# A fused attention and expert kernel on one core: in the second attention, the first output tile is issued ahead of two projections, the TensorE program is written without a loop, weights are split one step sooner, and VectorE rotates the first four parts by itself

## The reference

```python
q = jnp.einsum('bim,mhd->bhid', x, wq)      # 16 heads of 128, M = 256
k = jnp.einsum('bim,mhd->bhid', x, wk)
v = jnp.einsum('bim,mhd->bhid', x, wv)
q = rope(q)                                  # halves swapped, times sin, added to x times cos
k = rope(k)
s = jnp.einsum('bhid,bhjd->bhij', q * mult, k * mult)
s = s - INFTY_APPROX * mask                  # causal
p = jax.nn.softmax(s, axis=-1)
o = jnp.einsum('bhij,bhjd->bhid', p, v)
r = jnp.einsum('bhid,hdm->bim', o, wo)
```

## Time and profile before

| what | value |
|---|---|
| time, median of 3 runs | 1659.39 us (1657.05 to 1661.87) |
| the profiled execution, its own time | 1657.26 us |
| its span, first to last instruction | 1655.4 us |
| mean granted TensorE clock | 0.977 |
| attention B, first to last instruction of its own | about 745 to 1356 us of the span |
| busy over the span | PE 93%, PEld 80%, DVE 67%, ACT 49%, POOL 39% |

### The profile page before, as it was taken

One profiled execution on the slowest core, in us unless ns is written; L12 is line 12 of the kernel. 1 busy time (PEld: TensorE's weight loads), 2 busy tenths in 40 slices (PEclk: granted clock), 3 DMA queues, 4 the chain that ended last, 5 costly groups with the idle time before them and its releaser, 6 DMA issues. The chain is left out here.

```text
span 1655.4 us, 28360 instructions
## 1 busy us (share of the span) xinstructions
PE 1532.2 (93%) x9400; PEld 1322.7 (80%) x9400; DVE 1102.1 (67%) x2592; ACT 813.9 (49%) x2012; POOL 637.6 (39%) x550
## 2 busy tenths in 40 slices
PE   6699999999799999997999998998999978999998
PEld 4588888888678888876788887887888867888887
DVE  6577777777775555566667776766767787555554
ACT  3366666666542333325656655565666623333332
POOL 2676777776400000006555665565656600000000
PEclk9799999999999999998999999999999999999999
DMA  2100000000010000001443333333342321000001
GB/s 94 54 16 16 17 16 15 16 0 1 1 65 20 20 20 19 0 1 58 121 129 89 103 99 103 103 93 97 103 121 77 94 60 39 20 20 20 19 1 51
DMA packets 33727, 83.18 MB, mean 50 GB/s; under 512 B 3649, under 2 KB 24129, under 8 KB 33601
## 3 DMA queue, kind: packets, MB, share of 16 engines
q1 hardware_dynamic: 33600, 81.62, 16.0%
HBM read 54.34 MB, written 27.26 MB: 49 GB/s over the span
## 5 line engine op out<-in xcount | busy, mean ns | idle before, releaser
L378 POOL TENSOR_TENSOR ab_swapped<-ab_swapped,const 128x512 f32<-128x512 f32 x128 | 164.4, 1285 | 223.6 <-ACT ab_swapped L373 223.6
L1620 DVE TENSOR_TENSOR f_hidden<-ps,f_silu 128x512 f32<-128x512 f32 x128 | 87.7, 689 | 202.0 <-PE ps L116 202.0
L1510 ACT ACTIVATE f_silu<-ps 128x512 f32<-128x512 f32 x128 | 76.3, 598 | 283.0 <-PE ps L116 283.0
L114 PE MATMUL ps<-xh,f_wl 128*128 128x512 f32 x512 | 203.2, 397 | 1.5 <-DVE f_hidden L1620 1.5
L115 PE MATMUL ps<-xl,f_wh 128*128 128x512 f32 x512 | 202.8, 396 | 0.0
L116 PE MATMUL ps<-xh,f_wh 128*128 128x512 f32 x512 | 202.6, 396 | 0.0
L1339 POOL TENSOR_TENSOR ab_qk<-ab_qk,ab_swapped 128x512 f32<-128x512 f32 x128 | 175.2, 1369 | 10.0
L1229 DVE SCALAR_TENSOR_TENSOR x<-ps,ab_inv,x 128x256 f32<-128x256 f32 x256 | 120.0, 470 | 79.7 <-PE ps L116 74.9
L73 POOL TENSOR_TENSOR rstd<-shifted,minus_half 128x4 f32<-128x4 f32 x16 | 17.1, 1066 | 355.8 <-DVE shifted L67 355.7
L1107 ACT ACTIVATE ab_probs<-ab_probs,ab_negmax 128x128 f32<-128x128 f32 (+1 forms) x256 | 114.6, 448 | 76.7 <-DVE ab_negmax L1205 71.9
L626 ACT ACTIVATE aa_probs<-ps,aa_negmax 128x256 f32<-128x256 f32 x256 | 119.4, 473 | 60.4 <-DVE aa_negmax L709 52.8
(11 more groups left out here) (187 smaller groups left out, 4497.7 us busy)
## 6 DMA issues: line engine op xcount, KB each, us to landing
ab_scratch<-ab_squares SPq DMA_DIRECT2D x32, 768.0 KB, 3.3
ab_probsT<-ab_scratch SPq DMA_DIRECT2D x128, 192.0 KB, 3.8
f_stage<-wf_in SPq DMA_DIRECT2D x16, 768.0 KB, 4.2
b_stage<-wb_qkv_in SPq DMA_DIRECT2D x8, 768.0 KB, 5.8
a_stage<-wa_in SPq DMA_DIRECT2D x8, 608.0 KB, 3.7
x<-x_in SPq DMA_DIRECT2D x4, 512.0 KB, 6.9
bo_stage<-wb_out_in SPq DMA_DIRECT2D x8, 256.0 KB, 4.5
out<-x SPq DMA_DIRECT2D x4, 512.0 KB, 2.9
```

The costliest lines, as they stand in the source:

```text
L114: nc.tensor.matmul(out, ll, rh, start=start, stop=False)
L378: return engine.tensor_tensor(by_batch(out), by_batch(src), table(c, rows, col), ALU.mult)
L1620: nc.vector.tensor_tensor(hidden[:, m, :], UP(m), silu[:, m, :], ALU.mult).then_inc(hid_done, 1)
```

## The change

Five edits, all in `attention_b`:

1. In TensorE's `step`, output tile j - 2 is issued ahead of the two projections at j = 2 (at j = 3 nothing moves).
2. TensorE's eight pairs are written out in Python instead of the hardware loop. GpSimd's loop over the pairs is written out too. ScalarE keeps its loop.
3. Weight splits move: ScalarE's three from j = 3 to j = 2 of the same slot, VectorE's from j = 1 of the slots 1, 2 and 3 to j = 3 of the slots 0, 1 and 2.
4. The first four parts (slot 0) go to four PSUM banks of their own (3, 4, 5 and 2) and TensorE does not wait between them. VectorE rotates them without ScalarE: one product with cosines and two crosswise products with sines on 64 rows (`first_rope`). GpSimd subtracts. The waits `rope_read` and `swap_done` on TensorE begin with the fifth part, and the first projection of values waits for `swap_done` 4, since it writes bank 2.
5. In the start-up VectorE splits the first weights ahead of the layer norm's statistics, and the four `first_rope` stand between the pieces of the norm.

```diff
+        FIRST = [c.ps[:, bank, :] for bank in (3, 4, 5, 2)]
...
-                after(pe, rope_read, 4 * n + i - 1)
-                after(pe, swap_done, 4 * n + i - 1)
+                if n > 0:
+                    pe.wait_ge(rope_read, 4 * n + i - 1)
+                    pe.wait_ge(swap_done, 4 * n + i - 1)
...
+                if j >= 2 and not (first and s == 0):
+                    output(*later(it, half, s, -1), j - 2)
                 if j == 2 and not (last and s >= 1):
                     for i in (0, 1):
                         project(*later(it, half, s, 3), i)
-                if j >= 2 and not (first and s == 0):
-                    output(*later(it, half, s, -1), j - 2)
...
+            pe.wait_ge(swap_done, 4)
             project_values(0, 0, 0, 0)
...
-            head_pair(0, 0)
-            with pe.Fori(0, HP // 2 - 1) as two:
-                head_pair(2 * two + 1, 1)
-                head_pair(2 * two + 2, 0)
-            head_pair(HP - 1, 1)
+            for it in range(HP):
+                head_pair(it, it % 2)
...
-                if s == 0 and j == 3 and not last:
+                if s == 0 and j == 2 and not last:
                     split_hi(it + 1, 1 - half, 0)
...
-            for i in range(4):
-                swap(0, 0, i)
...
+            def first_rope(i):
+
+                dve.wait_ge(proj_ready, i + 1)
+                times_table(nc.vector, c, qk[:, 0, i, :], FIRST[i], ALL_ROWS, C_COSB).then_inc(rope_read, 1)
+                after(dve, rotated, i - 1)
+                times_table(nc.vector, c, swapped[0:64, i % 2, :], FIRST[i][64:128], slice(64, 128), C_SINB)
+                times_table(nc.vector, c, swapped[64:128, i % 2, :], FIRST[i][0:64], slice(0, 64), C_SINB).then_inc(swap_done, 1)
...
-                if s >= 1 and j == 1 and not last:
-                    if s < NG - 1:
-                        split_lo(it + 1, 1 - it % 2, s - 1)
+                if s < NG - 1 and j == 3 and not last:
+                    if s < 2:
+                        split_lo(it + 1, 1 - it % 2, s)
                     else:
                         split_wo(it + 1, 1 - it % 2)
...
+            split_lo(0, 0, 0)
             norm_stats(nc, c, own_norm, dve, 2)
-            split_lo(0, 0, 0)
+            split_lo(0, 0, 1)
+            first_rope(0)
             norm_rows(nc, c, own_norm, dve, 2)
-            split_lo(0, 0, 1)
+            first_rope(1)
             norm_stats(nc, c, own_norm, dve, 3)
-            for i in range(4):
-                rope(0, 0, i)
+            first_rope(2)
             norm_lo(nc, c, own_norm, dve, 2, own_banks)
+            first_rope(3)
```

More of the change, by code:

```diff
@@ L1127, in step @@
                     exps(*moved(it, s, j, LEAD))
-                if s == 0 and j == 3 and not last:
+                if s == 0 and j == 2 and not last:
                     split_hi(it + 1, 1 - half, 0)
-                if s == 1 and j == 3 and not last:
+                if s == 1 and j == 2 and not last:
                     split_hi(it + 1, 1 - half, 1)
-                if s == 2 and j == 3 and not last:
+                if s == 2 and j == 2 and not last:
                     split_wo(it + 1, 1 - half)
@@ L1328, in _, with rotate @@
             pool.wait_ge(own_norm.rstd_done, NG)
-            with pool.Fori(0, HP) as it:
-                for s in range(NG):
-                    for i in range(4):
-                        m = 4 * (it * NG + s) + i
-                        pool.wait_ge(swap_done, m + 1)
-                        rows, other = qk[:, s % 2, i, :], swapped[:, i % 2, :]
-                        times_table(nc.gpsimd, c, other, other, ALL_ROWS, C_SINB).then_inc(sin_done, 1)
-                        pool.wait_ge(sin_done, m + 1)
-                        pool.wait_ge(rope_read, m + 1)
-                        nc.gpsimd.tensor_tensor(rows, rows, other, ALU.add).then_inc(rotated, 1)
+            for i in range(4):
+                pool.wait_ge(swap_done, i + 1)
+                nc.gpsimd.tensor_tensor(qk[:, 0, i, :], qk[:, 0, i, :], swapped[:, i % 2, :], ALU.subtract).then_inc(rotated, 1)
+            def rotate(n):
+                for i in range(4):
+                    m = 4 * n + i
+                    pool.wait_ge(swap_done, m + 1)
+                    rows, other = qk[:, n % 2, i, :], swapped[:, i % 2, :]
+                    times_table(nc.gpsimd, c, other, other, ALL_ROWS, C_SINB).then_inc(sin_done, 1)
+                    pool.wait_ge(sin_done, m - 3)
+                    pool.wait_ge(rope_read, m + 1)
+                    nc.gpsimd.tensor_tensor(rows, rows, other, ALU.add).then_inc(rotated, 1)
+            for n in range(1, NG * HP):
+                rotate(n)
             for s in range(NG):
```

2 lines of the change are left out of this document (1 added, 1 removed).

## The result

Four runs of the changed kernel gave a median of 1608.49 us (1606.67 to 1610.53), four of the kernel before on the same chip 1658.41 us (1657.05 to 1661.87). The ratio is 0.9696 (0.9677 to 0.9716): 49.9 us less, where 47.9 were forecast. The profiled execution took 1610.53 us, its span 1608.8.

The account below looks back on a forecast made before the run. TensorE, busy 93% of the span, was taken to set the time. Gains of 27.2, 8.1, 11.05 and 1.5 us summed to 47.9, taken from the 1659.39 us median to give 1611.5 us, range 1605 to 1625.

Parts of the forecast that it names:

- Part 1: Attention B's slots: with output tile 0 ahead of the projections, TensorE's wait before tile 2 goes; 27.2 us over 28 slots.
- Part 2: Slots with a weight split: splitting sooner removes TensorE's seven waits for split weights; 8.1 us gained.
- part 3: TensorE's loop over the pairs written out: both jumps back and the lower clock behind them go; 11.05 us gained.
- The split behind `mixed_lo`: VectorE's moved split at s = 0, j = 3 delays what is queued behind it by up to 0.8 us; costs nothing.
- ScalarE's jump: The jump back of ScalarE's kept loop: taken as nothing, at most 3.9 us each, 7.8 us as the far end.
- Parts 4 and 5: Attention B's start-up, with banks of its own and an earlier first split: first mix some 1.5 us sooner, 1.5 us gained.
- a first mix later than 790.85: Sign in the profile after, at attention B's first mix, that would show the forecast wrong; about 789 was expected.
- Walking the string of VectorE with these durations, I get the fourth done at about 763.3: Start-up: VectorE's fourth part done at about 763.3, the seventh projection at 767 instead of 768.63.
- TensorE starts some 0.9 us sooner: Start-up: the first split no longer stands behind the statistics, so TensorE begins some 0.9 us before its former 748.83.
- A new wait in each slot: Rival: slack ahead of tile 2 or tile 0 fails and TensorE waits for VectorE again, half as long; 1625 us, chance 0.12.
- ScalarE's jump or a worse start-up: Rival: ScalarE's loop jump shows on the path at two places, 1619 us, or the start-up loses; chance 0.09.
- Standing at fetches: Rival: TensorE's written-out program is fetched too slowly in pairs 3 to 7, 5.5 us a stand, 1677 us; chance 0.03.

Follow-up runs that it names:

- the order alone: The kernel before with only output tile 0 put ahead of the two projections at j = 2; 1620.95 us, ratio 0.9785.
- old start: The changed kernel with edits 4 and 5 undone, so with the start-up of the kernel before; 1606.07 us, ratio 0.9693.
- split first: The changed kernel with the start-up of before, in that only the first weight split moved ahead of the norm's statistics; 1607.89 us, ratio 0.9703.
- spare turn: The changed kernel with one more, unread VectorE transposition of 128x384 at every step j = 3; 1611.54 us, ratio 0.9726.

## Why the prediction was right, and where its terms were not

The mechanism was the forecast one and the range held: three stalls of TensorE went and nothing took their place. Term by term:

- **Part 1, 27.2 us forecast, 31.4 measured.** The wait went, as it should, with the 0.2 us of slack ahead of tile 2 that were worked out (0.23 measured). Mis-sized was what comes back. The sum charged 0.10 for the slow matmul behind the mix and 0.04 for a later start, less 0.08: the step of the mix and the projections takes 4.82 us before and after, so the move costs nothing. The step of tile 2 went from 5.25 to 4.16. A slot lost 1.12, not 0.97, and 28 of them 31.4.
- **Part 2, 8.1 us forecast, 2 to 3 for the edit itself.** All edits together took 8.4 from these slots, so the sum holds, but the terms were not independent: the order alone takes 4.6 of it, since it puts work ahead of the waiting projection, and 1.1 us of what the slots with a jump had above a usual one, which had stood under part 3. The working priced each edit against the kernel before, never against the kernel with part 1 in it.
- **The split behind `mixed_lo`** was costed at nothing, and costs nothing (66.07 us in four slots). But splits last longer at their new place: the longest of `ab_wl` is 2.28 us, the median 1.57, where they were 1.94 and 1.14. The prediction set aside the rule of the Trainium skill, SBUF — State Buffer, in its section on the two sides of the memory, that a VectorE instruction with two SBUF inputs and one of GpSimd that reads SBUF lock each other out for a whole instruction. Its reason was that the longest row lay below the 2.6 us that the rule could give (1.2 and a GpSimd instruction of 1.37). That was the wrong comparison. A split of 128x1024 takes 1.22 us with GpSimd idle. VectorE and GpSimd in after, where it meets GpSimd:

```profile
870.12 2.09 DVE L1187 TENSOR_TENSOR ab_wl<-b_stage,ab_wh 128x1024 fp32r<-128x1024 f32 x1
```

```profile
869.84 1.30 POOL L378 TENSOR_TENSOR ab_swapped<-ab_swapped,const 128x512 f32<-128x512 f32 x1
871.21 2.16 POOL L1350 TENSOR_TENSOR ab_qk<-ab_qk,ab_swapped 128x512 f32<-128x512 f32 x1
```

GpSimd's instruction had 1.0 us left when the split started, and the split took that and 1.1 more; GpSimd's next, 1.3 us by itself, took 2.16 until 1.2 behind the split's end. The other rows fit too: 0.5, 0.9 and 1.2 us left go with 1.57, 1.94 and 2.28. So the trace agrees with the rule, in rows 7 already, and I was not entitled to discard it. The price of nothing holds because of the slack, not because the splits are not held.
- **Part 3, 11.05 us forecast, 9.9 for the edit itself;** the remaining 1.1 went already with the order alone, where the low clock behind the first jump was shorter. ScalarE's jump cost nothing, being 0.05 us.
- **Parts 4 and 5, 1.5 us gained forecast, 0 to 0.5 lost measured** (508.56 and 508.03 in all against 508.06 with the old start, less than the medians can tell). Here the prediction failed, by its own sign too, "a first mix later than 790.85". The step: "Walking the string of VectorE with these durations, I get the fourth done at about 763.3". Its end came at 767.2. The working took GpSimd's subtraction as ready when its inputs were; GpSimd's own queue had the second root of the norm ahead of it, which waits for VectorE's statistics of the last group, behind two rotated parts. That is 1.87 us of VectorE standing. With GpSimd's order mended the first mix comes at 45.95, still not sooner than 45.25, so a second step failed as well: "TensorE starts some 0.9 us sooner" is true, but the 1.38 us for which VectorE then stands ahead of the split were left out, and in the old start they make the first mix 1.5 us later (split first). The first mix was forecast at about 789 and came at 793.91, of which 1.5 us is a stage before that ended later in this execution.
- **The rivals.** A new wait in each slot, 0.12: none came, and the spare turn shows that 0.3 to 0.4 us stood between. ScalarE's jump or a worse start-up, 0.09: the start-up did lose instead of gain, but by about 1 us at most and not the rival's 7.8. Standing at fetches, 0.03: TensorE's program ran straight through eight pairs without a stand of its own.

That the sum came within 3 us of the median, and 1.2 of the profiled execution, is partly luck: part 1 was 4.2 us too small, and against it stand the start-up (2.5 from forecast to measured against the kernel before, slot 0 counted in), the later end of the stage before (1.5) and the stretch of low clock behind attention B (1.4). The last two are chance of that execution: the changed kernel's second one reached attention B 1.3 us sooner, had no such stretch, and its span was 1604.2 us instead of 1608.8.

## What to carry to other kernels

When TensorE is over 90% busy, ask where in a period the consumer idles and what the producer could have made in that time: here six matmuls moved ahead of twelve gave 36 of 50 us. Price several edits in sequence, each against the kernel with the earlier ones in it, and for each instruction given to another engine look at what stands ahead of it in that engine's own queue, not only at its inputs. An instruction moved to the front must be ready there: if it is not, the engine stands, and all that it used to do meanwhile comes later. Before writing a loop out or in, read the sequencer's branch row: it says whether a jump costs 0.05 us, 0.2 or nearly 4.

## What the runs showed of the hardware that was not expected

- A loop's jump back on TensorE took 0.21 to 0.25 us with bodies of 1513 traced instructions and fewer, and 3.55 to 3.88 with 1811 or 1812. On leaving the loop the same branch took 0.08. ScalarE's jump back took 0.05.
- A VectorE split with two SBUF inputs took what was left of GpSimd's running instruction and 1.1 us on top: 1.57, 2.10 and 2.28 us, against 1.22 with GpSimd idle.
- A bank that comes free just in time costs without showing as a wait: with `add_out` ending 0.06 us ahead of tile 2 instead of 0.23, tile 2's first matmul takes 0.22 until the next instead of 0.12, with no idle time before it in the trace (the spare turn).
- `normed`, VectorE's instructions of 128x256 from SBUF to SBUF, took 1.38 us for four apart from GpSimd's product and 2.45 where the first of them started beside it.
- Around the first mix, which comes behind a wait of 3.0 to 4.0 us, the granted clock was low for 3.4 us in some kernels and 6.8 in others that differ only in the start-up; in the latter it fell while TensorE still stood.
